# Two-layer graph network: weights' setup and transposes of h interleaved with the first block of neighbour products

## What is computed

```python
h = relu(layernorm(x))                       # first layer
mask = adj > 0
agg = mask @ h / max(deg, 1)
x = x + relu(concat(h @ W_self + b_self, agg @ W_nb + b_nb) @ W_comb + b_comb)
h = relu(layernorm(x)); state = h            # second layer, five steps
for _ in range(5):
    a_in  = adj   @ (state @ in_W.T + in_b)
    a_out = adj.T @ (state @ out_W.T + out_b)
    r, z  = sigmoid([a_in, a_out, state] @ r_W.T + r_b), sigmoid(... z_W, z_b)
    h_hat = tanh([a_in, a_out, r * state] @ h_W.T + h_b)
    state = (1 - z) * state + z * h_hat
out = x + tanh(state @ o1_W.T + o1_b) @ o2_W.T + o2_b
```

## Time and profile before

| | |
|---|---|
| runs | 1286.91, 1286.82, 1285.99 us; median 1286.82 |
| the profiled execution | 1285.99 us; its span 1284.2 us, mean granted TensorE clock 0.994 |
| TensorE, VectorE, ScalarE, GpSimd busy | 98%, 54%, 22%, 0% of the span |
| HBM | read 146.29 MB, written 35.13 MB |

### The profile page before, as it was taken

The page is one execution under the profiler, slowest core; times in us unless marked ns, Lnnn a source line. Parts: engine busy times, 40 slices in busy tenths (PEclk is TensorE's granted clock), DMA queues, the critical chain, the costliest instruction groups (busy, mean ns, idle before and its releaser), DMA issues.

```text
span 1284.2 us, 12914 instructions
## 1 busy us (share of the span) xinstructions
PE 1261.0 (98%) x4970; PEld 613.2 (48%) x4970; DVE 697.2 (54%) x1182; ACT 280.1 (22%) x544; POOL 3.0 (0%) x9
## 2 busy tenths in 40 slices
PE   7999999999998999999999999999999999999998
PEld 5666554444443444444444444444444444444445
DVE  5577654164746366177546428635624762661664
ACT  4755211011023012022202103211111330210111
POOL 0000000000000000000000000000000000000000
PEclk9999999999998999999999999999999999999999
DMA  8444092024481910830570380074066029116201
GB/s 299 150 163 165 28 369 102 1 87 175 168 339 54 349 56 21 306 131 1 197 262 0 130 298 31 19 288 152 0 231 228 0 76 346 37 35 227 86 0 66
DMA packets 42810, 182.19 MB, mean 142 GB/s; under 512 B 3457, under 2 KB 11906, under 8 KB 27010
## 3 DMA queue, kind: packets, MB, share of 16 engines
q1 hardware_dynamic: 41744, 177.62, 38.3%
q0 software_dynamic: 720, 3.67, 0.7%
q10 hardware_dynamic: 290, 0.14, 0.0%
HBM read 146.29 MB, written 35.13 MB: 141 GB/s over the span
## 4 chain that ended last, share of the span: by engine, by line
PE 89%; DVE 1%; issue 0%; ACT 0%; DVEq 0%
PE bank L298 87%; PE bank L461 1%; PE bank L414 0%; DVE work L1187 0%; DVE ST L1189 0%; DVE H L1034 0%; DVE work L1185 0%; PE bank L367 0%; DVE DR L1002 0%; DVE work L1162 0%; DVE work L1166 0%; DVE AT L991 0%; DVE res L1380 0%; DVE stat L941 0%; PE bank L387 0%
## 5 line engine op out<-in xcount | busy, mean ns | idle before, releaser
L298 PE MATMUL bank<-slot,LF 128*128 128x512 f16 x1792 | 391.1, 380 | 0.0
L298 PEld LDWEIGHTS bank<-slot,LF 128*128 128x128 f16 x1792 | 175.9, 98 | 211.4 <-issue 4.5
L298 PE MATMUL bank<-X,W 128*128 128x512 f32 x384 | 176.5, 592 | 0.0
L298 PE MATMUL bank<-ST,WG 128*128 128x512 f32 x320 | 148.4, 592 | 0.0
L298 PE MATMUL bank<-XT,W 128*128 128x512 f32 x288 | 135.3, 592 | 0.0
L298 PEld LDWEIGHTS bank<-X,W 128*128 128x128 f32 x384 | 72.7, 190 | 87.7 <-issue 86.6
L298 PE MATMUL bank<-work,WG 128*128 128x512 f32 x224 | 97.1, 592 | 0.0
L298 PE MATMUL bank<-AT,SN 128*128 (+1 forms) x256 | 97.0, 379 | 0.0
L298 PE MATMUL bank<-A,SN 128*128 (+1 forms) x256 | 97.0, 379 | 0.0
L298 PEld LDWEIGHTS bank<-ST,WG 128*128 128x128 f32 x320 | 60.8, 190 | 75.2 <-issue 74.6
L298 PEld LDWEIGHTS bank<-XT,W 128*128 128x128 f32 x288 | 54.5, 190 | 67.4 <-issue 66.2
(11 more groups left out here) (158 smaller groups left out, 1225.2 us busy)
## 6 DMA issues: line engine op xcount, KB each, us to landing
slot<-quad_d SPq DMA_DIRECT2D x112, 1024.0 KB, 5.3
WG<-in_adj SPq DMA_DIRECT2D x32, 512.0 KB, 4.3
quad_d<-AT SPq DMA_DIRECT2D x14, 1024.0 KB, 5.0
quad_d<-A SPq DMA_DIRECT2D x14, 1024.0 KB, 6.3
SN<-in_x SPq DMA_DIRECT2D x2, 1024.0 KB, 10.6
x_d<-SN POOLq DMA_DIRECT2D x4, 512.0 KB, 2.9
x1o<-x_d SPq DMA_DIRECT2D x1, 2048.0 KB, 8.5
out<-res SPq DMA_DIRECT2D x4, 512.0 KB, 3.0
```

Of the source, the lines that this page charges most:

```text
L298: return pe.matmul(o, l, r, start=start, stop=stop, skip_group_check=again)
```

## The change

The bias columns: GpSimd multiplies wgR by the bias columns on each partition, adds the two halves into `scaled`, and TensorE then sums over partitions with 12 one-column matmuls against ones instead of 24 against `col`; they go to bank 6, bias0 to bank 7. turn_h(q) moves out of the setup into the first block's rounds 5, 7, 9, 11, into banks 6 and 7, and its copies out stand four rounds later. mean_sum(0, 4, 8, 12) wait for one quarter of h each; high(q) (ScalarE), low(q) and normal(q) (VectorE) of the later quarters stand in rounds 2, 5, 8. The relu pass of VectorE goes: normal writes SCALE times the normalised value, and high, low and the copies of the transposed h apply the relu. A one-element square root early on ScalarE brings the table load forward.

```diff
@@ -35,6 +35,8 @@
 H2_AT = 12
+HIGH_AT = [2, 5, 8]
+TURN_AT = [5, 7, 9, 11]
...
 def graph_net(nc, x, adj, w_in, w_out, wg_t, w0_t, w_comb, w_o, cols, b_comb, o2_b, consts, out):
@@ -133,6 +135,8 @@
         h32 = AT[:, 1, :, :].rearrange("p t n -> p (t n)").bitcast(FP32).rearrange("p (t d) -> p t d", t=NT)
+        scaled = AT[:, 2, :, :].rearrange("p t n -> p (t n)").bitcast(FP32)[:, 0:4 * GATES].rearrange(
+            "p (w j n) -> p w j n", w=2, j=2)
         fusedS = AT[:, 3, :, :].rearrange("p t n -> p (t n)").bitcast(FP32)[:, 0:4 * GATES].rearrange(
...
@@ -152,6 +156,8 @@
         setup_done = sem("setup_done")
+        w12_sum, gsum, gcol_out = sem("w12_sum"), sem("gsum"), sem("gcol_out")
+        warm = sem("warm")
         var_ready, sqrt_ready = sem("var_ready"), sem("sqrt_ready")
...
         h_hi, h_lo = sem("h_hi"), sem("h_lo")
@@ -284,6 +290,15 @@
         def _(pool):
+            pool.wait_ge(ld_c, 48)
+            for w in range(2):
+                pool.wait_ge(ld_w[w], 32)
+                for j in range(2):
+                    nc.gpsimd.tensor_scalar(scaled[:, w, j, :], wgR[w][:, j, :], col[:, 2 * w + j:2 * w + j + 1], None,
+                                            ALU.mult).then_inc(gsum, 1)
+                pool.wait_ge(gsum, 3 * w + 2)
+                nc.gpsimd.tensor_tensor(scaled[:, w, 0, :], scaled[:, w, 0, :], scaled[:, w, 1, :],
+                                        ALU.add).then_inc(gsum, 1)
             pool.wait_ge(fused_out, 8)
...
             for b in range(NB):
@@ -312,14 +327,14 @@
                 pe.wait_ge(h_ready, b + 1)
-                if b < 2:
-                    pe.wait_ge(fused_out, 2 * b + 6)
+                if b == 0:
+                    pe.wait_ge(gcol_out, 1)
                 else:
-                    pe.wait_ge(hT_act, b - 1)
-                    pe.wait_ge(hT_dve, b - 1)
+                    pe.wait_ge(hT_act, b)
+                    pe.wait_ge(hT_dve, b)
                 for f in range(FT):
                     for q in range(BT):
-                        last = pe.transpose(bank[4 + 2 * (b % 2) + f][:, q * P:q * P + P],
+                        last = pe.transpose(bank[6 + f][:, q * P:q * P + P],
                                             h32[:, BT * b + q, f * P:f * P + P], ident)
...
@@ -331,32 +346,27 @@
                                   wcR[:, 2 * w + j, :], j == 0, j == 1)
+            last.then_inc(w12_sum, 1)
             pe.wait_ge(left_ready, 1)
+            pe.wait_ge(fused_out, 8)
             for j in range(4):
-                mm(bank[2][:, 0:D], L0[:, j, :], wcR[:, j, :], j == 0, False)
-            mm(bank[2][:, 0:D], cst[0:1, C_ONE:C_ONE + P], b_combR[0:1, :], False, True)
-            turn_h(0)
-            turn_h(1)
-
+                mm(bank[7][:, 0:D], L0[:, j, :], wcR[:, j, :], j == 0, False)
+            mm(bank[7][:, 0:D], cst[0:1, C_ONE:C_ONE + P], b_combR[0:1, :], False, True)
+
+            pe.wait_ge(gsum, 6)
             for w in range(2):
                 for t in range(6):
-                    for j in range(2):
-                        last = mm(bank[3][:, 6 * w + t:6 * w + t + 1], wgR[w][:, j, t * P:t * P + P],
-                                  col[:, 2 * w + j:2 * w + j + 1], j == 0, j == 1)
+                    last = mm(bank[6][:, 6 * w + t:6 * w + t + 1], scaled[:, w, 0, t * P:t * P + P],
+                              cst[:, C_ONE:C_ONE + 1], True, True)
             last.then_inc(setup_done, 1)
-            turn_h(2)
-            turn_h(3)
...
                 pe.wait_ge(conv, 4 * (4 * b + m // 4 + 1))
-                if i == 2:
-                    pe.wait_ge(w12_out, 1)
                 if i == 0:
                     pe.wait_ge(id16_ready, 1)
-                    pe.wait_ge(hT_act, NB)
-                    pe.wait_ge(hT_dve, NB)
+                    pe.wait_ge(fused_out, 8)
                 if i >= 3:
...
                         pe.wait_ge(at_act, (i - 3) // 2 + 1)
@@ -370,9 +380,10 @@
                 pe.wait_ge(mask_ready, i + 1)
+                if m % BT == 0 and b == 0:
+                    pe.wait_ge(h_hi, m // BT + 1)
+                    pe.wait_ge(h_lo, m // BT + 1)
                 if m == 0 and b == 0:
-                    pe.wait_ge(h_hi, 4)
-                    pe.wait_ge(h_lo, 4)
                     pe.wait_ge(w12_out, 1)
...
                     pe.wait_ge(agg_act, b)
@@ -392,6 +403,9 @@
                 pe.wait_ge(agg_dve, b + 1)
+                if b == 0:
+                    pe.wait_ge(hT_act, NB)
+                    pe.wait_ge(hT_dve, NB)
                 if b > 0:
...
                     pe.wait_ge(s_dve, b)
@@ -418,6 +432,8 @@
                 mean_sum(i)
+                if i in TURN_AT:
+                    turn_h(TURN_AT.index(i))
                 if i % NT == H2_AT and i > NT:
...
                 if i + LEAD < NT * NB:
@@ -747,6 +763,8 @@
+            act.wait_ge(warm, 1)
+            nc.scalar.activation(nrm[:, 2, 0:1], nrm[:, 3, 0:1], ACT.Sqrt)
             for e in range(4):
...
                     act.wait_ge(fused_ready, 2 * e + part + 1)
@@ -757,22 +775,27 @@
                     convert(k, r)
-            for q in range(4):
+
+            def high(q):
                 act.wait_ge(h_ready, q + 1)
-                copy(hi_lo[:, BT * q:BT * q + BT, 0, :], h32[:, BT * q:BT * q + BT, :], SCALE).then_inc(h_hi, 1)
+                nc.scalar.activation(hi_lo[:, BT * q:BT * q + BT, 0, :], h32[:, BT * q:BT * q + BT, :],
+                                     ACT.Relu).then_inc(h_hi, 1)
+
             def move_h(q):
                 act.wait_ge(hT_ready, q + 1)
-                copy(ST[:, 0, q * BN:q * BN + BN], bank[4 + 2 * (q % 2)][:, :]).then_inc(hT_act, 1)
-
-            move_h(0)
-            move_h(1)
-            act.wait_ge(setup_done, 1)
+                nc.scalar.activation(ST[:, 0, q * BN:q * BN + BN], bank[6][:, :], ACT.Relu,
+                                     scale=1.0 / SCALE).then_inc(hT_act, 1)
+
+            def combined():
+                act.wait_ge(setup_done, 1)
+                copy(gcol[:, :, :].rearrange("p w t -> p (w t)"), bank[6][:, 0:12])
+                copy(bias0, bank[7][:, 0:D]).then_inc(gcol_out, 1)
+
+            high(0)
+            act.wait_ge(w12_sum, 1)
             for w in range(2):
-                copy(W12[:, 2 * w:2 * w + 2, :].rearrange("p k n -> p (k n)"), bank[w][:, :])
-            copy(gcol[:, :, :].rearrange("p w t -> p (w t)"), bank[3][:, 0:12])
-            copy(bias0, bank[2][:, 0:D]).then_inc(w12_out, 1)
-            move_h(2)
-            move_h(3)
+                ins = copy(W12[:, 2 * w:2 * w + 2, :].rearrange("p k n -> p (k n)"), bank[w][:, :])
+            ins.then_inc(w12_out, 1)
...
@@ -799,12 +822,20 @@
                 k = 2 * (i // 4 + 1) + i % 4 // 2
+                if i == 0:
+                    move_adj(0)
                 if k < 8 * NB:
...
                     block_end(i // NT - 1)[0]()
-                if i % 2 == 0:
+                if i % 2 == 0 and i:
                     move_adj(i)
+                if i == 1:
+                    combined()
+                if i in HIGH_AT:
+                    high(HIGH_AT.index(i) + 1)
+                if i - 4 in TURN_AT:
+                    move_h(TURN_AT.index(i - 4))
                 if i >= NT and i % NT in STAGE_AT:
...
             sums, root, state, turned = block_end(NB - 1)
@@ -948,6 +979,7 @@
+            v.memset(nrm[:, 3, 0:1], 1.0).then_inc(warm, 1)
             row_stats(range(NT), 0)
...
             dve.wait_ge(ld_c, 48)
@@ -966,22 +998,32 @@
                 link(v.reciprocal(rs, sc))
-
-            newton(NT, 1)
-            for q in range(4):
+                return rs
+
+            rs = newton(NT, 1)
+            link(v.tensor_scalar(rs, rs, SCALE, None, ALU.mult))
+
+            def normal(q):
                 for t in range(BT * q, BT * q + BT):
...
                                           ALU.subtract, ALU.mult)
-                link(ins)
-                hq = h32[:, BT * q:BT * q + BT, :].rearrange("p t d -> p (t d)")
-                v.tensor_scalar(hq, hq, 0.0, None, ALU.max).then_inc(h_ready, 1)
-            for q in range(4):
+                ins.then_inc(h_ready, 1)
+
+            def low(q):
+                dve.wait_ge(h_ready, q + 1)
                 dve.wait_ge(h_hi, q + 1)
                 v.scalar_tensor_tensor(out=hi_lo[:, BT * q:BT * q + BT, 1, :], in0=h32[:, BT * q:BT * q + BT, :],
-                                       scalar=SCALE, in1=hi_lo[:, BT * q:BT * q + BT, 0, :],
-                                       op0=ALU.mult, op1=ALU.subtract).then_inc(h_lo, 1)
+                                       scalar=0.0, in1=hi_lo[:, BT * q:BT * q + BT, 0, :],
+                                       op0=ALU.max, op1=ALU.subtract).then_inc(h_lo, 1)
+
+            def turned_h(q):
                 dve.wait_ge(hT_ready, q + 1)
-                v.tensor_copy(ST[:, 1, q * BN:q * BN + BN], bank[5 + 2 * (q % 2)][:, :]).then_inc(hT_dve, 1)
```

(12 more changed lines are left out.)

## The result

The changed kernel takes 1289.92 us (median of 15 runs, 1289.12 to 1290.59) against 1287.01 for the kernel before, run beside it (15 runs): +2.9 us, ratio 1.0021, 95% interval 1.0013 to 1.0029. The interval leaves out 1, and 2.9 us is just over the 2.6 us that the prediction named as what can be told from no change. The profiled execution has a span of 1287.5 us, 3.3 more than that of before.

What follows compares the result with a forecast made beforehand. TensorE, busy 98%, was the bound, with the written ScalarE and VectorE order deciding the first block. -11.2 + 5.2 + 3.0 + 2.2 + 3.44 - 0.2 = +2.4, clock +1.2, Relu +0.3: +3.9, 1290.7 us; range 1285.5 to 1295.5.

Steps and rivals of the forecast that it cites:

- The sign: Whole kernel: slower by over 0.2%, chance 0.69.
- the three joins: First block's loop: VectorE's low waits for ScalarE's late high and delays products 1, 4 and 7.
- Part 1: Prologue: bias passes take 2.6 us, GpSimd is hidden, product 0 starts at 28.5 instead of 39.71: -11.2 us.
- Part 2: Transposes of h after products 5, 7, 9, 11: four times 0.86 us, +3.44 us before product 15.
- Part 3: Stalls ahead of products 1, 4 and 7 in the first block: 5.2, 3.0 and 2.2 us.
- rival (c): First block: quarters overlap, joins dissolve, faster; 1279 us without stalls, 1284 with half of them; chance 0.12.
- Part 4: Clock falls in the 5.2 us stall, product 1 runs at 1.2 GHz: +1.2 us; shorter stalls cause no fall.
- Rival (d): Clock also falls or stays low over the second and third stalls: 1294 to 1296.5 us; chance 0.11.
- Part 5: Relu for Copy on ScalarE: each of three highs on a chain 0.1 us longer, +0.3 us, bounds 0 and 0.4.
- That the shift would reach the end: Behind product 15: untouched code keeps TensorE full, so product 15's shift should reach the end.
- rival (b): Joins cost as worked out, clock holds, Relu costs what Copy does: +2.4 us, 1288 to 1289.2; chance 0.19.
- (e): Prologue: GpSimd's sums come late, at 5 us an operation 4.4 us later, 1295 us; chance 0.04.

Runs made afterwards that it cites:

- the second profile: The changed kernel run again unedited for another profiled execution: 1289.95 us (9 runs).
- The two kernels with the highs early: Changed kernel with normal(2), normal(3), high(1), high(2) ahead of the loop; lows after VectorE's masks 1280.08 us, lows ahead of them 1280.76 us.
- the ballast: Changed kernel with eight unused fp16 matmuls behind round 0's adjacency transposes, in the wait for product 1: 1289.88 us, ratio to before 1.0026.
- the kernel with the splits ahead of the loop: Changed kernel with normal(2), normal(3), high(1), high(2) ahead of the loop, lows after mask and move: 1280.08 us, ratio to before 0.9946.
- transposes in the waits: Changed kernel with the transposes of h behind products 0, 3, 6, 9 instead of 5, 7, 9, 11: 1287.70 us, ratio to before 1.0002.
- columns in the loop: The kernel with the splits ahead of the loop, with the bias columns moved behind product 3: 1283.26 us (8 runs).
- lows behind the masks: Changed kernel with VectorE's low and normal after mask and move in rounds 2, 5, 8: 1286.89 us, ratio to before 0.9998.
- two ballasts: The ballast kernel with ten more unused matmuls behind round 3's transposes, in the wait for product 4: 1290.14 us (9 runs).
- GpSimd's sums alone: Kernel before with only GpSimd forming the sums and 12 one-column matmuls instead of 24: 1286.74 us, ratio to before 0.9996.

## Why the prediction was right, and where it was off

The sign, the three joins and the order of size held: +3.9 us forecast, +2.9 measured. That the total came so close is partly luck. At product 15 the shift was 4.85 us, 1.0 more than forecast, and 5.5 in the second profile; behind it 1.5 us went that the forecast had let reach the end.

- **Part 1.** The passes took 2.6 us as worked out (25.65 to 28.24 for the weight loads). The prologue as a whole ended 1.2 us later than in the profile of before (25.65 against 24.42), though nothing in it had changed: the matmuls started 0.3 us later on their DMA (6.33 against 6.01), and the weight loads of the fused products went over from 0.34 to 0.19 us each at about 12 us instead of 11; the granted clock reads 1.00 in both, so the cause of that stays open. In the second profile of the same kernel it ended at 24.23. So it varies from one execution to the next, and product 0's 29.85 for 28.5 is mostly that. GpSimd was hidden, at 1.8 to 2.2 us an operation.
- **Part 2.** 0.91 us for each transposition of a quarter, not 0.86: 3.65 us for 3.44.
- **Part 3.** From the first adjacency transpose to product 1 7.69 us, worked out 7.85. In the second profile it was 7.89. From product 1 to 4, 7.57 and 7.58 in the two profiles, forecast 7.8; from 4 to 7, 6.72, forecast 6.7. The waits themselves were shorter than the 5.2, 3.0 and 2.2 of the sum, 3.77, 2.10 and 2.07: TensorE was slow at products 0 to 2 and filled part of the first two, which changes no start. The forecast places for products 1, 4 and 7, 35.0, 42.8 and 49.5, stand in the second profile as 35.03, 42.61 and 49.33. The two kernels with the highs early show that these chains turned a gain into a loss: without them the change is 6 to 7 us faster than the kernel before, not 3 slower. The sum of rival (c) without stalls was -8.0.
- **Part 4.** The +1.2 us for product 1 is shown (7.57 us to product 4, 6.52 with the ballast), but the step that led to it is not what happened: the prediction had the 5.2 us stall let the clock fall, and it fell before the stall, at 29.5 and 26.7 in the two profiles, during or just behind the one-column passes. In the kernel with the splits ahead of the loop it fell at 29.0, and with the passes moved ahead of W12 there, nothing else changed, it did not fall. The prediction had read the same in the kernel before (30.7, in the passes) and did not carry it over. That a wait can do it by itself is shown where the transposes stand in the waits: back at 30.9, the clock fell at 34.3, inside a wait of 3.04 us. The step that failed outright is that stalls of 3.0 and 2.2 us, being shorter than 4.1, would not let the clock fall. It did in six profiles: inside waits of 3.04 (transposes in the waits) and 3.09 us (columns in the loop), and behind waits of 2.79 (one ballast), 1.99 (lows behind the masks), 2.07 (two ballasts) and 2.07 us (the changed kernel once more). The clock also outlived such waits, of 2.10 and 2.07 us in the first profile of the changed kernel and of 2.07 with one ballast, so the length of a wait doesn't settle it. The row I took the bound from shows one fall, and no row of before has a wait between 0.9 and 5.7 us. Rival (d) had this as its mechanism; of the changed kernel's two profiles it struck in one, and at one wait.
- **Part 5.** Relu costs what Copy does: high took 1.04 to 1.06 us, 1.06 before, move_h 0.58 to 0.6. The +0.3 us should have been 0. There was no further table load. By the Trainium skill (ScalarE: Activation LUTs, Table sets: the hidden batching unit) relu lies in every set; the trace agrees here.
- **That the shift would reach the end.** It did not in full, and this is the larger miss. In the first profile the shift is 4.85 us at product 15, 4.79 at the third block's dense product (122.38 against 117.59), 4.43 at the fourth's (150.59 against 146.16), where the kernel before had small waits that the changed one does not have, 4.44 at 402 us, and 3.3 at the end. The last 1.1 us went at the 5.73 us wait of the second layer:

```profile
401.99 1.97 PE L477 MATMUL bank<-cst,ST 128*128 128x128 f32 x8 [5.73 <-DVE ST L1237]
...
410.40 7.93 PE L313 MATMUL bank<-slot,LF 128*128 128x512 f16 x36
```

From its end to the third run of matmuls are 8.41 us here, 9.54 in the kernel before, and 9.21, 8.32 and 8.94 in the kernels with the lows behind the masks, with one ballast and with the transposes in the waits. Over all thirteen profiles the same code takes 8.32 to 9.84 us, by when the clock came back (2.95 us after work resumed here, 5.23 in the kernel before), and from the third run to the end of the span all thirteen take 877.1 us within 0.05. So the rest of the kernel is untouched and the whole of this difference is the clock's. Whether the change has a part in it stays open: both profiles of the changed kernel have the short time (8.41, 8.38), but the kernel with two ballasts, whose wait ended as late (402.79), took 9.70. The profile of before lies 1.0 us under the median of its 15 runs and the first of the changed kernel 0.6 under its own, which is why the spans differ by 3.3 and the medians by 2.9.

The rival (b), that the clock holds and Relu is free, was wrong in its first half and right in its second; (c) was excluded by the written order, as said; (e) did not occur. What the early square root and the dropped relu pass are worth no run tells apart.

## What to carry to other kernels

Work put into a loop "where the engine has time" holds up everything queued behind it on that engine, for as long as its own input is late: before moving a step between two engines, walk both queues and see that the producer's half stands well ahead of the consumer's. Look first for time ahead of the loop in which both engines are idle. Here ScalarE had 3.4 us of it free and VectorE 3.8, and using it turned +0.2% into -0.5%.

## What the runs showed of the hardware that was not expected

- The clock fell behind waits of only 2 to 3 us, and after work had resumed: at 43.3 with the wait ended at 42.39, at 50.6 after 49.33, at 49.9 after 49.48, at 36.8 after 35.58. Other waits of 2.07 and 2.10 us it outlived. With one wait filled the fall came behind the next, with two behind the third, in one profile of each.
- One-column passes with a full weight load each let it fall while TensorE was busy: in the second profile of the changed kernel TensorE and its weight loads were busy 100% from 26 to 27 us, and it fell at 26.7. With the same passes at the start of the W12 product and dense matmuls behind them it held.
- Transposes alone brought the clock back a second time. With GpSimd's sums alone, TensorE did nothing but fp32 transposes from 32.75 to 36.1 us, and the clock rose at 35.6:

```profile
34.00:35.00 1.00, 1.00 (x7) 0.83 (x6) 1.00 (x2) 0.53 (x2) 0.00 (x0) 0.50 0.00 0
35.00:36.00 1.00, 1.00 (x7) 0.86 (x5) 1.00 (x3) 0.32 (x1) 0.00 (x0) 0.69 0.00 0
```

- On GpSimd the multiplication of 768 fp32 elements by a column took 2.20 us, longer than the addition of two tensors of that size, 1.81.
